# Moving a router's gating block and four silus within a six-stage transformer kernel

## The reference

```python
# mixture of experts (8 experts, the best 2 per token)
router_logits = x_flat @ router_w.T
top_k_logits, top_k_idx = jax.lax.top_k(router_logits, TOP_K)
router_probs = jax.nn.softmax(top_k_logits, axis=-1)
hidden = jnp.square(jax.nn.relu(jnp.einsum('nc,ecd->ned', x_flat, w1_all)))
out_all = jnp.einsum('ned,edc->nec', hidden, w2_all)
...
# feed-forward: x, the hidden values and the weights are rounded in blocks of 16
gate = fp4_linear(x, w_gate)
y = fp4_linear(x, w_up)
h = jax.nn.silu(gate) * y
return fp4_linear(h, w_down)
```

## Time and profile before

| | |
|---|---|
| time, median of 3 runs | 733.61 us (731.99 to 733.76) |
| span of the profiled execution | 731.5 us |
| the execution's time outside the span | not recorded by itself; the median less the span is 2.1 us |
| PE busy | 662.0 us (90% of the span) |
| DVE busy | 592.4 us (81%) |
| ACT busy | 454.1 us (62%) |
| POOL busy | 309.0 us (42%) |
| moe_a, about | 14 to 145 us of the span |
| linatt, about | 145 to 272 us |
| moe_b, about | 270 to 395 us |
| ffn_a, about | 395 to 500 us |

### The profile page before, as it was taken

How to read it: one execution, slowest core, us unless ns; L and a number is a source line. 1 busy time by engine, 2 the same in 40 slices (tenths; PEclk the granted TensorE clock), 3 DMA queues, 4 the chain that set the end, 5 groups by cost and what they waited for, 6 DMA issues and landing times.

```text
span 731.5 us, 16089 instructions
## 1 busy us (share of the span) xinstructions
PE 662.0 (90%) x5826; PEld 476.2 (65%) x5826; DVE 592.4 (81%) x1546; ACT 454.1 (62%) x862; POOL 309.0 (42%) x425
## 2 busy tenths in 40 slices
PE   4999999889999989999997799989999987889995
PEld 2777776667788777777775365656567555556564
DVE  2788878846667578988778799999899999899983
ACT  3777777766466318777787467656644424676642
POOL 5000022055655511001104467736567568577520
PEclk9999999989999989999999699999999999999998
DMA  8000000000000000000000000000000000000001
GB/s 213 23 0 0 0 1 0 2 2 4 3 0 2 4 2 1 0 1 1 0 2 0 1 0 1 0 1 1 1 2 1 0 1 1 1 29 16 29 15 29
DMA packets 13465, 7.14 MB, mean 10 GB/s; under 512 B 1176, under 2 KB 13408, under 8 KB 13408
## 3 DMA queue, kind: packets, MB, share of 16 engines
q1 hardware_dynamic: 11328, 5.33, 2.7%
q10 hardware_dynamic: 2080, 1.05, 0.5%
HBM read 4.28 MB, written 2.10 MB: 9 GB/s over the span
## 4 chain that ended last, share of the span: by engine, by line
PE 73%; ACT 11%; DVE 7%; issue 4%; POOL 3%; DMA 0%; DVEq 0%; POOLq 0%; ACTq 0%
PE ps L1486 68%; PE ps L1888 2%; DVE x_sb L1119 2%; ACT ffn_work L553 2%; ACT ffn_work L754 2%; PE ps L1494 1%; ACT ffn_work L591 1%; ACT xnT L604 1%; ACT x_sb L864 1%; ACT hqT L860 1%; PE ps L1500 1%; ACT ffn_work L586 1%; POOL shared L416 1%; DVE stats L1020 1%; POOL rstd L366 1%
## 5 line engine op out<-in xcount | busy, mean ns | idle before, releaser
L1486 PEld LDWEIGHTS ps<-w_sb,sq_h 128*128 128x128 f32 x1024 | 131.3, 191 | 70.8 <-ACT sq_h L623 51.6
L1119 DVE SCALAR_TENSOR_TENSOR x_sb<-ps,gates,x_sb 128x128 f32 (+1 forms) x512 | 147.0, 343 | 21.3 <-PE ps L1486 17.1
L1486 PE MATMUL ps<-w_sb,sq_h 128*128 128x128 f32 x1024 | 137.3, 277 | 3.4 <-ACT sq_h L623 3.3
L1486 PE MATMUL ps<-xnT,w_sb 128*128 128x512 f32 x256 | 133.4, 604 | 0.0
L361 POOL TENSOR_SCALAR vareps<-meanvar 128x4 f32<-128x4 f32 (+1 forms) x28 | 8.9, 319 | 245.3 <-DVE meanvar L1029 244.8
L619 ACT ACTIVATE relu_h<-ps 128x512 f32<-128x512 f32 x128 | 75.6, 590 | 56.9 <-PE ps L1486 56.5
L623 ACT ACTIVATE sq_h<-relu_h 128x512 f32<-128x512 f32 x128 | 80.6, 630 | 4.2
L1486 PE MATMUL ps<-gateT,xnT 128*128 128x352 f32 x128 | 58.4, 540 | 17.4 <-ACT ffn_work L754 13.2
L408 POOL TENSOR_TENSOR shared<-shared 128x128 f32<-128x128 f32 x112 | 51.0, 455 | 27.9 <-ACT shared L713 19.8
L597 ACT ACTIVATE xn<-x_sb,shift,rstd 128x128 f32<-128x128 f32 (+1 forms) x136 | 57.1, 481 | 6.6 <-POOL shift L369 5.7
L1486 PE MATMUL ps<-downT,hqT 128*128 128x128 f32 x384 | 57.0, 286 | 4.2 <-ACT hqT L860 4.0
(11 more groups left out here) (168 smaller groups left out, 1354.5 us busy)
## 6 DMA issues: line engine op xcount, KB each, us to landing
x_sb<-in_L_attn_x_dram SPq DMA_DIRECT2D x8, 256.0 KB, 7.0
out_dram<-x_sb SPq DMA_DIRECT2D x8, 256.0 KB, 2.3
w_sb<-in_L_ffn_w_all_dram ACTq DMA_DIRECT2D x2, 512.0 KB, 6.0
wraw<-in_L_attn_qkv_w_dram SPq DMA_DIRECT2D x1, 192.0 KB, 4.9
wraw<-attn_in_proj_weight_dram SPq DMA_DIRECT2D x1, 192.0 KB, 3.8
fraw<-in_L_ffn_w_down_dram SPq DMA_DIRECT2D x1, 176.0 KB, 3.0
fraw<-in_L_ffn_w_gate_dram SPq DMA_DIRECT2D x1, 128.0 KB, 2.7
fraw<-in_L_ffn_w_up_dram SPq DMA_DIRECT2D x1, 128.0 KB, 2.5
```

Source lines behind the costliest of these rows:

```text
L1119: t = nc.vector.scalar_tensor_tensor(tile_b(i, j), bank(4 + e % 4, TPB, C)[:, j, :], gates[:, j, e:e + 1], tile_b(i, j), ALU.mult, ALU.add)
L1486: return nc.tensor.matmul(o, a, b, start=start, stop=stop, **kw)
```

## The change

Three edits and a swap. On ACT, `gate_exp(i)` moves from after expert 2's square to after expert 0's. On DVE, `gating(i + 1)` becomes one block, issued ahead of the four accumulations of expert 7. In DVE's last body of moe_b, `gating_end` is issued ahead of `x_scales`. On ACT in ffn_a, all four silus of group 0 are issued ahead of `x_squares` and `x_offsets` of group 1. No instruction is added or taken away.

```diff
--- before.py
+++ after.py
@@ -621,7 +621,7 @@
 
                         act.wait_ge(s["down_done"], i * E + e + 1)
                         nc.scalar.activation(sq_h[:, e % 2, :], relu_h[:, e % 2, :], ACT.Square).then_inc(s["sq_ready"], 1)
-                        if e == 2 and (first or type(i) is not int or i > 0):
+                        if e == 0 and (first or type(i) is not int or i > 0):
                             gate_exp(i)
                         if e == 5 and not first and type(i) is int and i == 0:
 
@@ -904,11 +904,10 @@
                         evac_xnT(s, g + 2)
 
                 if first:
-                    silu(s, 0, 0)
+                    for j in range(TPB):
+                        silu(s, 0, j)
                     x_squares(s, 1)
                     x_offsets(s, 1)
-                    for j in range(1, TPB):
-                        silu(s, 0, j)
                 normal(s, first, 2)
                 evac_xnT(s, 1)
                 for g in range(GROUPS):
@@ -1067,30 +1066,26 @@
             def moe(s, nxt, tile_n, first):
                 ch = Chain(dve, s["dve_chain"])
 
-                def gating(i, between):
+                def gating(i):
 
 
                     tb = tiebreak[:, :, :].rearrange("p a b -> p (a b)").unsqueeze(1).to_broadcast([P, TPB, E * E])
                     df = diff[:, :, :, :].rearrange("p j a b -> p j (a b)")
                     dve.wait_ge(s["logits_done"], i + 1)
                     copied = ch.add(nc.vector.tensor_copy(logits[:, :, :], bank(router_bank(first, i), TPB, E)))
-                    between(0)
                     ch.need(copied)
                     ch.add(nc.vector.tensor_reduce(top[:, :], logits[:, :, :], AX, ALU.max))
                     for j in range(TPB):
                         l = logits[:, j, :]
                         compared = ch.add(nc.vector.tensor_tensor(diff[:, j, :, :], l.unsqueeze(1).to_broadcast([P, E, E]),
                                                                   l.unsqueeze(2).to_broadcast([P, E, E]), ALU.subtract))
-                    between(1)
                     ch.need(compared)
                     nc.vector.tensor_tensor(ex[:, :, :], logits[:, :, :],
                                             top[:, :].unsqueeze(2).to_broadcast([P, TPB, E]),
                                             ALU.subtract).then_inc(s["sub_ready"], 1)
                     lifted = ch.add(nc.vector.scalar_tensor_tensor(df, df, TIE, tb, ALU.mult, ALU.add))
-                    between(2)
                     ch.need(lifted)
                     ahead = ch.add(nc.vector.tensor_scalar(df, df, 0.0, None, ALU.is_gt))
-                    between(3)
                     ch.need(ahead)
                     ch.link(nc.vector.tensor_reduce(rank[:, :, :], diff[:, :, :, :], AX, ALU.add))
 
@@ -1105,10 +1100,10 @@
                                                            ALU.mult, ALU.mult))
 
                 def body(i, more, ahead):
+                    if first or type(i) is not int or i > 0:
+                        gating_end(i)
                     if not first and not more:
                         x_scales(nxt, ch, 0)
-                    if first or type(i) is not int or i > 0:
-                        gating_end(i)
 
                     def accumulate(e, j):
                         if j == 0:
@@ -1123,10 +1118,9 @@
 
                     for e in range(E):
                         if e == E - 1 and more:
-                            gating(i + 1, lambda j: accumulate(E - 1, j))
-                        else:
-                            for j in range(TPB):
-                                accumulate(e, j)
+                            gating(i + 1)
+                        for j in range(TPB):
+                            accumulate(e, j)
                         if more and e == (5 if ahead else 4):
 
                             dve.wait_ge(s["xn_ready"], i + 2)
@@ -1173,7 +1167,7 @@
                         dve.wait_ge(s["xn_ready"], 1)
                         ln_stats(s, ch, 1, TPB, tile_b)
                         dve.wait_ge(s_tie, 1)
-                        gating(0, lambda j: None)
+                        gating(0)
                         dve.wait_ge(s_x, 16 * (B - 2))
                         pre = ch.k
                     else:
```

## The result

| | before | after |
|---|---|---|
| time, median of 5 runs each, on one chip | 733.61 us (731.99 to 735.36) | 726.1 us (725.26 to 727.49) |
| span of the profiled execution | 731.5 us | 723.2 us |
| mean granted clock of PE | 0.974 | 0.981 |

The ratio is 0.9892, 95% interval 0.987 to 0.9915: faster by 7.9 us (6.2 to 9.5), where 5.2 were forecast. By the ratio, the time sits at 725.7 us, 0.1 under the forecast's low end of 725.8.

The account below looks back on a forecast made before the run. PE, busy 90% of the span, was taken as the bound, so the change pays only where PE stands still. 4.7 + 0.3 + 0.3 - 0.1 = 5.2 us took 733.6 to 728.4 us, range 725.8 to 730.8.

Parts of the forecast that it names:

- The silus, 4.7: Head of ffn_a: with all four silus first, DVE's product starts 4.7 us earlier, and the later offsets stay hidden.
- half pace: Rival, ffn_a's gate loop: clock falls to 1.2 GHz, 2.2 us of the gain is lost, 730.6; chance 0.12.
- no change: Rival, head of ffn_a: it does not wait for the silus; only moe's 0.5 us are left, 733.1; chance 0.06.
- The usual boundaries, nothing: 12 usual group boundaries: DVE gets ahead by about 2 us but then waits for PE; nothing counted.
- ACT idling in front of L614: Sign in the loop that the prediction is wrong; it had the exponential at expert 0 fit with 0.2 us over.
- The slower rival: Exponential at expert 0 becomes a wait, and late `ex` halts PE; at 1.3 us late, 737.1; chance 0.04.
- The end of moe_b, 0.3: `gating_end` ahead of `x_scales` and the early exponential bring accumulations forward; 0.3 us taken, bounds 0 and 0.46.
- The head of group 7 in moe_a, 0.3: DVE's run in group 6 starts 0.4 to 0.7 us sooner; net 0.15 to 0.45 at the next head, 0.3 taken.
- The case "More": ffn_a: the clock rises earlier behind the one gap left, 1 to 3 us more, 726.5; chance 0.16.
- The fifth case: Group 6 of moe_a: comparison reaches the ports before the memset, DVE's run starts 2 us or more sooner, 726.4; chance 0.05.

Follow-up runs that it names:

- the second of them: Kernel before with ten spare matmuls filling three PE waits, one in moe_a's last group and two in ffn_a: 732.1 us, ratio 0.9978.

## Why the prediction missed

**The silus, 4.7: right.** 4.72 by the profile, with the silus as far apart as forecast and the offsets hidden behind the product; half pace and "no change" fell. The 4.7 already held a clock term, as the rows of before there stand at the low clock: with the wait filled, the old order takes 8.14 us from silu to product (one profile), so 3.25 are order and 1.5 clock.

**The usual boundaries, nothing: right in moe_a.** Groups 1 to 5 take 78.00 us and the exponential waits at none of their boundaries. In moe_b it waits twice, by 0.49 and 0.72 us. The prediction named ACT idling in front of L614 as a sign of being wrong; it allowed 0.1 for the first boundary, and 0.2 were lost in groups 1 to 6. The slower rival's mechanism exists, as the exponential without the block showed, and the block removes it elsewhere.

**The end of moe_b, 0.3: too small.** 0.46, its upper bound. The block alone gave 0.33 of it, which the prediction had put down to the swap and the early exponential.

**The head of group 7 in moe_a, 0.3: the step that failed.** Two errors. First, I took 0.25 off for the exponential standing ahead of a relu at that head. It cost 0.05 (14.67 to 14.72 us for group 7), so the net is 0.7, over the bound of 0.45. PE's gap at the second `down` was 0.67, not 1.0, and the 1.54 at the next head fits the forecast. Second, and larger: the term priced the gap by its length alone, because in the one profile that I had, PE ran at full clock behind it. In the six profiles with a gap of 2.32 us or more there, group 7 took 16.10 to 16.14 us in five; only the first profile of before has 14.67. In the eight with 1.55 or less it took 14.67 to 14.74 every time, with the gap shortened by order, by an earlier memset or by filling alone. If executions divide as the profiles do, the shorter gap is worth another 1.4 us in five of six, 1.2 in the mean. The exponential at expert 1 shows that the length of the single wait matters, with DVE's order as in after. That the standing still brings the slow stretch, and not what stands in the queue, is best seen at the gap of 4.79 us in ffn_a: a slow stretch stands behind it in all ten profiles without spare matmuls and in none of the four with them. At group 7 the filling was profiled once, and one unfilled profile in six was fast too.

This 1.4 is shown in group 7, not in the whole time. No experiment times it alone, and linatt behind it took 120.8 us in the mean of the five profiles with the slow stretch and 121.9 in the nine without (119.7 to 124.4), so part of it may be handed back there.

The corrected sum is 4.7 + 0.7 + 0.46 - 0.2 + 1.2 = 6.9 us, inside 6.2 to 9.5, and its moe part of 2.2 is inside the 1.3 to 4.1 timed, while the 1.0 of order alone lies just below. The last 1.0 to the 7.9 is no more than the interval allows, and stays open. Part may be a clock gain elsewhere: the loss to the low clock fell to 13.6 us in the mean after, from 18.3. But that count does not convert into time at one rate: filling before took away 5.4 us of it and gave 1.6.

**The case "More"** named 726.5, about where the time fell, but by another place: it had the clock rise sooner behind the gap of 4.79, and that stretch stayed at 0.61. Its own 1 to 3 us reach down to 725.4, so the low end of 725.8 was 0.4 too high by the prediction's own figures; the 725.7 falls between the two. **The fifth case** did not happen: the copy came 0.38 us later than before, the memset 0.42 later, and the comparison arrived 0.37 behind it. The early memset has tried what it would bring, and its size of 2 us is borne out: 1.96 in group 6 by the profile, 2.0 by the times (724.1 against 726.1, with intervals that overlap a little).

The comparison took 3.28 us beside the memset and 0.29 free of it. With this the Trainium skill's exclusive lock (SBUF — State Buffer, "SBUF: two separate sides") agrees. But not every DVE instruction is held: in the kernel before, the tie-break (110.49) and an accumulation (110.82) ran beside the same memset in their usual 0.42 and 0.34 us. The Trainium skill's 2.66 us for a table switch (ScalarE: Activation LUTs, "What ACT_TABLE_LOAD costs") was too much here: the load takes 1.28 and the exponential follows 1.29 behind its start.

## What to carry to other kernels

Before pricing a wait of TensorE, look at what clock its matmuls have behind it in more than one profile: one profile may show full clock where five of six do not. And ask whether a wait could be divided: behind waits of 0.67 and 1.54 us no slow stretch stood in three profiles, behind one of 2.32 it did. An operation that one engine meets early must be made early on the other; moved alone it cost 3.1 us, the block alone gave nothing, and together (with the swap) they gave 2.7. A long GpSimd memset belongs where it does not meet a VectorE instruction that others wait for; but find out first whether that instruction sets the time: in the old order the same move gave nothing.

## What the runs showed of the hardware

Granted clock behind a wait of PE at the head of group 7: after 2.32 to 2.37 us it stood at 1.2 GHz in five of six profiles, after 1.55 or less in none of eight. Behind the wait of 4.79 us in ffn_a it stood at 1.2 GHz in ten of ten profiles, and in none of four with spare matmuls in that wait. A kernel with ten such products more became 1.6 us faster.

Slow stretches also move by themselves: over 255 to 270 us in linatt the granted clock was 0.77, 0.89 and 1.00 in three profiles of the same code, and when the head of linatt was filled, one stood at 164 us instead. So fillings do not add up. All four kernels with fillings lost less to the low clock than the kernel they were made from (11.0 us for 13.6, 13.0 for 18.4, 11.2 and 12.5 for 13.0, in the mean over their executions), but only the second of them was faster for it.
